# A causal attention kernel: SP's transposes in order of need, max products at the head of their share, PV seven steps behind

## The reference

```
y  = layernorm(x); z = rmsnorm(y) * rms_w
q, k, v = z @ w_in.T                      # 32 x 64, 8 x 64, 8 x 64
q, k = rope(q), rope(k)
o  = softmax(causal(q k^T / 8)) v         # per head, 4 heads share k and v
x2 = x + y + o @ w_out.T
u  = layernorm(x2)
out = x2 + u + (silu(u Wu^T) * (u Wg^T)) Wd^T      # Wu, Wg, Wd ternary-quantised
```

## Time and profile before

| what | value |
|---|---|
| median of 3 runs | 2386.37 us (2384.61 to 2387.1) |
| the profiled execution | 2387.29 us, span 2385.5 us |
| busy in the span | PE 2067.9 us, DVE 1576.6, POOL 1529.3, ACT 1059.8 |
| attention | from about 107 us to about 1800 us |
| mean granted TensorE clock | 0.959 of full speed |

### The profile page before, as it was taken

The page is one execution under the profiler, slowest core; times in us unless marked ns, Lnnn a source line. Parts: engine busy times, 40 slices in busy tenths (PEclk is TensorE's granted clock), DMA queues, the critical chain, the costliest instruction groups (busy, mean ns, idle before and its releaser), DMA issues. The chain is left out here.

```text
span 2385.5 us, 53908 instructions
## 1 busy us (share of the span) xinstructions
PE 2067.9 (87%) x17919; PEld 1247.4 (52%) x17919; DVE 1576.6 (66%) x2864; ACT 1059.8 (44%) x2352; POOL 1529.3 (64%) x1716
## 2 busy tenths in 40 slices
PE   2479988987998898799889879988998889999998
PEld 1245655554565555556555545655555444444443
DVE  8258857966885796689579668957975666222221
ACT  3235644654554555455455645554554332111110
POOL 5568887886888788678878867887881333212211
PEclk7789999998999999999999999999999999999999
DMA  5321121122112111211211131121115542000000
GB/s 162 116 53 33 33 50 41 32 47 50 33 33 50 41 33 33 64 32 33 48 35 33 38 66 34 33 48 35 33 35 186 160 159 75 1 18 9 9 18 18
DMA packets 228788, 122.77 MB, mean 51 GB/s; under 512 B 187168, under 2 KB 208416, under 8 KB 226976
## 3 DMA queue, kind: packets, MB, share of 16 engines
q1 hardware_dynamic: 228512, 119.26, 19.9%
HBM read 50.53 MB, written 25.17 MB: 32 GB/s over the span
## 5 line engine op out<-in xcount | busy, mean ns | idle before, releaser
L711 DVE TENSOR_REDUCE mpart<-a_ps 128x1 f32<-128x512 f32 (+3 forms) x1288 | 736.5, 599 | 211.3 <-PE a_ps L540 131.3
L623 ACT ACTIVATE p<-a_ps 128x512 f32<-128x512 f32 (+3 forms) x1283 | 663.1, 532 | 416.6 <-PE a_ps L555 239.5
L775 POOL TENSOR_TENSOR pl<-p 128x512 f16<-128x512 f32 (+2 forms) x641 | 626.5, 990 | 169.2 <-ACT p L623 168.4
L570 PE MATMUL a_ps<-v,p 128*128 128x129 f16 x4352 | 559.9, 224 | 107.1 <-POOL pl L775 63.1
L703 DVE TENSOR_TENSOR pl<-p 128x512 f16<-128x512 f32 (+1 forms) x642 | 556.9, 871 | 25.6 <-ACT p L623 25.1
L570 PEld LDWEIGHTS a_ps<-v,p 128*128 128x128 bf16 x4352 | 409.5, 99 | 251.9 <-issue 103.6
L572 PE MATMUL a_ps<-v,pl 128*128 128x65 f16 x4352 | 524.0, 195 | 0.0
L537 PE MATMUL a_ps<-k_hl,q_hh 128*128 128x512 f16 (+3 forms) x1288 | 448.8, 355 | 63.3 <-issue 27.0
L554 PE MATMUL a_ps<-q_hh,k_hl 128*128 128x512 f16 (+3 forms) x1283 | 456.7, 356 | 54.0 <-DMA q_lm<-qk_lo 51.8
L555 PE MATMUL a_ps<-q_lm,k_h 128*128 128x512 f16 (+3 forms) x1283 | 455.9, 355 | 0.0
L572 PEld LDWEIGHTS a_ps<-v,pl 128*128 128x128 f16 x4352 | 398.8, 99 | 84.9 <-issue 6.7
(11 more groups left out here) (101 smaller groups left out, 3021.8 us busy)
## 6 DMA issues: line engine op xcount, KB each, us to landing
attn_scratch<-onorm SPq DMA_DIRECT2D x32, 512.0 KB, 3.1
p_att<-attn_scratch SPq DMA_DIRECT2D x64, 256.0 KB, 3.5
raw<-ffn_t SPq DMA_DIRECT2D x12, 1024.0 KB, 6.5
wraw<-w_in_t SPq DMA_DIRECT2D x9, 768.0 KB, 5.1
resid_scratch<-xin SPq DMA_DIRECT2D x4, 1024.0 KB, 4.3
raw<-w_out_t SPq DMA_DIRECT2D x1, 4096.0 KB, 15.0
x<-resid_scratch SPq DMA_DIRECT2D x4, 1024.0 KB, 6.8
out<-x SPq DMA_DIRECT2D x16, 256.0 KB, 2.0
```

Source lines behind the costliest of these rows:

```text
L570: nc.tensor.matmul(o, p_high[:, i % RING, t * P:(t + 1) * P], v[:, par, j, 0:VU], start=(j == 0 and t % 2 == 0), stop=False, skip_group_ch ...
L623: nc.scalar.activation(p32[:, i % RING, r * P:CHUNK], sbank(i)[:, r * P:CHUNK], ACT.Exp, scale=SCALE).then_inc(exp_done, 1)
L711: nc.vector.reduce_max(mpart[:, u % 2, t, kk:kk + 1], side_bank(part, ("piece", ahead, u, i))[:, 0:width], AX.X)\
L775: nc.gpsimd.tensor_tensor(pl[:, i % RING, cols], p32[:, i % RING, cols], p_high[:, i % RING, cols], ALU.subtract).then_inc(low_pool, 1)
```

## The change

`PV_LAG` becomes 7, so `OUT_LAG` becomes 5; the ring stays at 10. The pieces of a unit are dealt so that in a longer unit than the one that hosts it the doubled steps come first (2, 1, 2, 1 in place of 1, 2, 1, 2; and 2, 1, 1 in place of 1, 1, 2), and the four pieces of units 0 and 1 in a host of 16 steps stand at its steps 0, 4, 8, 12 in place of 3, 7, 11, 15. An "hh" is not issued earlier than 8 steps before its first piece. Stores move back by 4 to 13 steps. The prologue takes the first head's queries and the keys first.

```diff
-PV_LAG = 5
+PV_LAG = 7
...
-            pieces = [(ahead, w, i) for i in range(j * m // n, (j + 1) * m // n)]
+            pieces = [(ahead, w, i) for i in range(m) if i * n // m == j]
...
-    timed = [(FIRST_STEP[2] + 2, ("store", 3, -1))]
-    timed += [(FIRST_STEP[HG * (c + 1)] + OUT_LAG + 4, ("store", c, 0)) for c in range(NCH - 1)]
+    timed = [(FIRST_STEP[4] - 2, ("store", 3, -1))]
+    timed += [(FIRST_STEP[HG * (c + 1) + 1] + 4, ("store", c, 0)) for c in range(NCH - 1)]
...
             free = FIRST_STEP[before + 1] + 1
-            timed.append((max(n + QK_LOW_LAG + 1, free), ("hh", c, h, ahead)))
+            wanted = UNITS * ahead + HG * c + h - 2
+            wanted = STEPS * (wanted // UNITS) + FIRST_STEP[wanted % UNITS]
+            timed.append((max(n + QK_LOW_LAG + 1, free, wanted - 8), ("hh", c, h, ahead)))
...
+            query_high(0, 0, 0, 0)
+            keys(0, 0, 0, 0)
+            query_high(0, 0, 1, 0)
+            query_low(0, 0, 0, 0)
+            for h in range(2, HG):
+                query_high(0, 0, h, 0)
+            keys(0, 1, 0, 0)
             for h in range(HG):
-                query_high(0, 0, h, 0)
-            keys(0, 0, 0, 0)
-            query_low(0, 0, 0, 0)
-            for h in range(HG - 1):
-                query_high(0, 1, h, 0)
-            keys(0, 1, 0, 0)
+                if ("hh", 1, h, 1) in TRANSFERS:
+                    query_high(0, 1, h, 0)
```

More of the change, by code:

```diff
@@ L489, in _ @@
                 for h in range(HG):
-                    sp.wait_ge(hh_in[c][h], 16 * 2 * GROUPS + (16 if c == 0 or h < HG - 1 else 0))
+                    sp.wait_ge(hh_in[c][h], 16 * 2 * GROUPS + (16 if ("hh", c, h, 1) in TRANSFERS else 0))
                     sp.wait_ge(lm_in[c][h], 16 * 2 * GROUPS + (16 if c == 0 and h == 0 else 0))
```

## The result

The changed kernel takes 2395.93 us (median of 6 runs, 2392.18 to 2401.51) where the kernel before takes 2386.73 in the same comparison (2384.61 to 2387.8): a ratio of 1.0041, 95% interval 1.0028 to 1.0054. It is slower by 9 us. Forecast were 2316, so the prediction is wrong by 80 us and in its sign.

The account below looks back on a forecast made before the run. PE was held by a late "lm" before step 32, POOL in steps 8 to 26, full POOL or DVE later. 8.3 us a group times 8, with the prologue 71 us, off 2387.3 gave 2316; 8-in-10 range 2285 to 2348.

Parts of the forecast that it names:

- The three places: PE's stop before step 32 on a late "lm"; POOL as pacemaker in steps 8 to 26; POOL or DVE full later.
- SP's order, 4.0 us a group: Before step 32: moving "hh" behind the wanted transposes lets SP issue lm 6 4.0 us earlier in every group.
- First eight steps neutral: Steps 0 to 8 of a group: two short PVs leave them, but lm 2 hangs on the maxima; no gain or loss.
- PV and unit_out, steps 8 to 26, 2.0 us: Running both two steps later closes POOL's waits for projection copies; its last low half comes 2.0 us earlier per group.
- Steps 32 to 159, 2.2 + 0.3 us: Per group, 2.2 us gained in steps 40 to 127 (bounds 0 and 6) and 0.3 in the last two units.
- the rival of a freed PE: The lag removes PE's waits throughout: 6 us in steps 40 to 127, 13 a group; 2278 us, 15%.
- Pieces at the head: Dealing doubled steps first: same number and shapes, up to 0.8 us in odd groups inside the 2.2, nothing besides.
- Stores, prologue: Moved stores change nothing; in the prologue keys leave earlier and lm 1 goes out 4.8 us earlier.
- SP's order alone: Rival: only the 4.0 us a group before step 32 and the prologue's 4.8 are gained; 2350 us, 15%.
- The port rival: The shared SBUF port, or POOL and DVE, take all the later gain; 6.0 us a group remain: 2334 us, 20%.
- The clock rival: PE stays at half speed from step 26 to 40 after two stops, 11 us more a group; 2404 us, 4%.
- a new wait of the same size: Rival: transfers were hidden, or the lag makes an equal new wait, so nothing is gained; 2385 us, 3%.

Follow-up runs that it names:

- sp_order: Kernel before with only SP's new transfer order, stores and prologue; PV five steps behind and pieces dealt as before: 2366.37 us, ratio 0.9901.
- sp_out_4: sp_order, PV still five steps behind, with unit_out four steps behind (one later): 2344.32 us, ratio 0.9816.
- sp_lag_7: Changed kernel with the pieces dealt as before (PV seven steps behind, unit_out five): 2374.89 us, ratio 0.9947.
- sp_lag_7_out_6: sp_lag_7 with unit_out six steps behind in place of five: 2334.33 us, ratio 0.9782.
- changed_out_6: The whole changed kernel with unit_out six steps behind in place of five: 2362.73 us, ratio 0.9891.
- sp_lag_7_job_52: sp_lag_7 with the projections of steps 53 and 133 moved to 52 and 132, unit_out left at five: 2339.67 us, ratio 0.9799.
- sp_load_late: sp_order with the load of the next group's weights issued after lm 4, not ahead of the group's first transposes: 2348.45 us, ratio 0.9837.

## Why the prediction was wrong

**What bounds it now: right.** The three places were the right ones, and all three moved.

**SP's order, 4.0 us a group: the size read off was right, one neighbour was missed.** Steps 8 to 36 of sp_order are 4.7 us shorter, part of it clock. (The 1.3 us an issue fits the "hh", 5.47/4, and not the 3.3 us for two "k"; in the changed kernel the "k" took 1.19 and 1.26.) The failing sentence is "SP's other lm have no more in front of them than before: one hh each at the start of a group". The "hh" that moved behind the "k" of chunk 1, which waits for POOL, push the load and "lm 1" back; steps 0 to 8 paid 2.51 us, and the later load brought 18 us back in all. "First eight steps neutral" fails with it. That the moved "hh" are late for no piece was right.

**PV and unit_out, steps 8 to 26, 2.0 us: right, and for the reason given.** Both parts together were put at 6.0 us by step 32; group 3 shows 5.5, the waits at steps 12 and 17 gone, one of 1.18 near step 26 (forecast 3) and one of 4.36 before step 32 (forecast 4). The sum named the later `unit_out` as what closes POOL's holes, and sp_out_4 shows that it alone does; the lag of PV, under the same heading, was not needed for it.

**Steps 32 to 159, 2.2 + 0.3 us: the step that failed.** I saw the meeting with the jobs of steps 53 and 133 and priced it at one operation's wait: DVE's split of v, 1.8 us once. It did wait (2.51 us against the 1.86 of the earlier trace rows), but I did not follow the other two that hang on the same copy: the rotary products on POOL, with the normalise between them and their sum, and from there `qk_high_part` on ACT, with the exponentials behind it. The measured price is 33 us in the changed kernel and 35 to 41 in sp_lag_7, 4 to 5 us a group, where the sum had only that one wait of 1.8 us, set off within a gain of 2.2. The gain itself was too large as well: in sp_lag_7_out_6, with neither the meeting nor the new dealing, steps 32 to 160 are 0.7 us shorter, not 2.5. PE's own 63.1 us of waits for POOL went, as the rival of a freed PE had it, and came back as waits for the exponential.

**Pieces at the head: nothing. Wrong by 17 us alone,** 12 for the doubled steps and 5 for the spread ones, and by 21 in the changed kernel (against sp_lag_7). "Same number, same shapes" says nothing of the order on DVE, where the reduce is awaited in its place in the list with the low half and split behind it. None of the counts I used could show it; laying DVE's list against PE's for one step with a projection would have.

**Stores, prologue.** The first "k" leaves at 86.09 (forecast 87) and "lm" of unit 1 at 113.16 (forecast 114.7). The first scores start 5.6 us earlier in this trace; over the traces with the new prologue it is 3.6 to 6.0, so the 4.8 of the sum is of the right size. The stores alone were not tried.

**The rivals.** SP's order alone had 2350; it is 2366, for the missed neighbour. The port rival is not what happened, since closing the meeting gave time although POOL and DVE had the same work. Still DVE's low halves take 926 ns in the mean in the changed kernel, 895 in changed_out_6 and 868 in sp_lag_7_out_6, with equal shapes and count: 35 us of DVE's time between the first and the last over 642 operations. The Trainium skill (SBUF — State Buffer, SBUF: two separate sides) says that a DVE operation with two SBUF inputs and a GpSimd operation that reads SBUF hold a shared port pair for their whole length, and the other is blocked. Durations that shift with the order of the lists agree with that; no run here isolates it. And they don't set the time: sp_lag_7_job_52 has 924 ns and is 35 us faster than sp_lag_7. The clock rival named the right effect in the wrong place: not steps 26 to 40 but a new stop of 2.39 us before step 61. The 3% of "a new wait of the same size" was the case that came, and it held too little: three edits had been put at "neutral" or "nothing" by argument, and each was an order in some engine's list. The range was also narrower than the chances beside it: the rivals at 2350, 2278, 2404 and 2385 lie outside 2285 to 2348 and had 37% together, where the range left 20. An addition of the parts as measured alone (-21, +17.5, +17) gives +13 where +9 came.

## What to carry to other kernels

When a step is moved in an in-order queue, follow every consumer of what now comes later, and for each what stands queued behind it, to the engine that bounds; a meeting priced at one wait of 1.8 us cost 4 to 5 us a group. Change the distance of one kind of work at a time: one constant tied two (`OUT_LAG` to `PV_LAG`), and the gain lay in the one and the loss in where the pair landed. Before moving a wait-bound transfer, list what the same queue issues behind it, bulk loads too.

## What the runs showed of the hardware

- A transposing DMA issued behind a 768 KB load and an "hh" was used by PE 4.3 us after its issue (735.01 to 739.32 in sp_order) and took 4.2 us to land; behind three "hh" and no load it landed in 3.0 us (sp_load_late), and the "lm" of step 32 behind two "k" was used 2.5 us after its issue (790.55 to 793.08 in the changed kernel).
- Stops of PE of 0.4 to 1.9 us before step 32 left the granted clock at 2.4 GHz in six of the groups 1 to 7 of sp_order; with the seventh, of 2.7 us, came 3.4 us at 1.2 GHz. In sp_load_late, three of four stops of 1.9 to 2.5 us were followed by it. The 2.39 us before step 61 of the changed kernel is one of seven such, and all seven were. The length of a stop alone does not tell: in changed_out_6 the stop before step 151 has 1.9 us and all seven were followed by the low clock, while the one before step 26 has 2.5 us and two of seven were:

```profile
772.92 0.39 PE L559 MATMUL a_ps<-q_hh,k_hl 128*128 128x512 f16 x1 [2.54 <-ACT p L628]
```

So a stop's price can jump: a 128x512 matmul right after one took 0.62 us where the clock had fallen and 0.38 where it had not.
